# The third block's convolution filled and read three beats earlier in a hand-ordered Mamba and SwiGLU kernel

## The reference

```
x_in, res = split(x @ W_in)                    # 512 + 512 channels
u  = silu(causal_conv4(x_in))                  # 4 taps along the tokens, per channel
dt, B, C = split(u @ W_x)                      # 16, 16, 16
delta = softplus(dt @ W_dt + b_dt)
h[t] = exp(delta[t]*A) * h[t-1] + delta[t]*B[t]*u[t]      # 512 channels x 16 states
y[t] = sum over states of h[t]*C[t]  +  u*D
x1 = layernorm(x + (y * silu(res)) @ W_out)
out = layernorm(x1 + (silu(x1 @ Wg.T) * (x1 @ Wu.T)) @ Wd.T)      # hidden width 768
```

## Time and profile before

| what | us |
|---|---|
| median of 3 runs | 1822.53 |
| lowest and highest of them | 1819.36, 1822.55 |
| the profiled execution, its own time | 1828.11 |
| its span, first to last instruction | 1826.3 |
| mean granted TensorE clock | 0.990 |

### The profile page before, as it was taken

How to read it: one execution, slowest core, us unless ns; L and a number is a source line. 1 busy time by engine, 2 the same in 40 slices (tenths; PEclk the granted TensorE clock), 3 DMA queues, 4 the chain that set the end, 5 groups by cost and what they waited for, 6 DMA issues and landing times.

```text
span 1826.3 us, 32557 instructions
## 1 busy us (share of the span) xinstructions
PE 1692.8 (93%) x10128; PEld 1272.7 (70%) x10128; DVE 1683.3 (92%) x1958; ACT 1604.4 (88%) x2769; POOL 1606.6 (88%) x1629
## 2 busy tenths in 40 slices
PE   7979898999989899898999989899898999988788
PEld 3556676776767677676776767677676776767667
DVE  4989899999999999999999989999999999999994
ACT  4887989999898998989899898998989899898874
POOL 3989799998989899899998989999898998989870
PEclk9999999999999999999999999999999999999899
DMA  7312223222222223222232222313223232221110
GB/s 241 116 48 105 82 74 112 82 105 81 106 81 82 105 71 114 96 81 104 82 108 79 104 82 82 116 60 132 78 82 104 82 109 78 105 71 59 35 47 24
DMA packets 82108, 164.57 MB, mean 90 GB/s; under 512 B 10369, under 2 KB 28033, under 8 KB 81938
## 3 DMA queue, kind: packets, MB, share of 16 engines
q1 hardware_dynamic: 80498, 160.90, 25.5%
q10 hardware_dynamic: 1440, 1.58, 0.3%
HBM read 87.47 MB, written 8.91 MB: 53 GB/s over the span
## 4 chain that ended last, share of the span: by engine, by line
PE 74%; ACT 13%; POOL 4%; issue 4%; DVE 2%; DMA 1%; SPq 1%; DVEq 0%; ACTq 0%; POOLq 0%
PE ht_upper L737 11%; PE ht_lower L737 10%; PE y_upper L762 9%; PE fill L663 8%; PE fill L673 8%; PE fill L559 7%; PE fill L642 6%; POOL dbu L1237 3%; PE fill L612 3%; PE fill L595 3%; PE fill L574 3%; ACT gt L1103 2%; ACT da L1094 2%; DVE h L1432 2%; ACT z L988 2%
## 5 line engine op out<-in xcount | busy, mean ns | idle before, releaser
L1237 POOL TENSOR_TENSOR dbu<-du,brep 128x512 f32<-128x512 f32 x1024 | 1286.3, 1289 | 155.1 <-DVE h L1432 130.8
L1432 DVE TENSOR_TENSOR_SCAN h<-da,carry,dbu 128x512 f32<-128x512 f32 x960 | 1185.7, 1269 | 58.1 <-ACT da L1094 54.8
L1094 ACT ACTIVATE da<-delta,a_s 128x512 f32<-128x512 f32 x960 | 654.9, 692 | 78.2 <-DVE h L1432 71.2
L1103 ACT ACTIVATE gt<-ht_upper,ct 128x512 f32<-128x512 f32 x512 | 350.1, 684 | 69.7 <-PE ht_upper L737 66.5
L737 PE MATMUL ht_upper<-ident,h 128*128 128x128 f32 x2048 | 315.8, 277 | 70.4 <-ACT gt L1103 50.1
L737 PEld LDWEIGHTS ht_upper<-ident,h 128*128 128x128 f32 x2048 | 243.8, 142 | 196.0 <-issue 132.9
L1444 DVE SCALAR_TENSOR_TENSOR acc<-ht_lower,ct,acc 128x512 f32<-128x512 f32 x480 | 350.2, 730 | 14.9 <-PE ht_lower L737 13.4
L737 PE MATMUL ht_lower<-ident,h 128*128 128x128 f32 x2048 | 313.4, 276 | 26.1 <-DVE acc L1444 22.3
L762 PE MATMUL y_upper<-ident,gt 128*128 128x128 f32 x2048 | 309.7, 274 | 0.8 <-ACT kb L920 0.8
L737 PEld LDWEIGHTS ht_lower<-ident,h 128*128 128x128 f32 x2048 | 240.6, 142 | 79.2 <-DVE h L1432 37.7
L762 PEld LDWEIGHTS y_upper<-ident,gt 128*128 128x128 f32 x2048 | 246.4, 142 | 51.4 <-issue 38.2
(11 more groups left out here) (189 smaller groups left out, 1881.1 us busy)
## 6 DMA issues: line engine op xcount, KB each, us to landing
brep<-b_rows SPq DMA_DIRECT2D x127, 512.0 KB, 3.8
xs<-xin SPq DMA_DIRECT2D x242, 256.0 KB, 2.5
xr<-x SPq DMA_DIRECT2D x16, 512.0 KB, 5.4
xt_s<-x_t SPq DMA_DIRECT2D x15, 512.0 KB, 3.8
out<-xr SPq DMA_DIRECT2D x15, 512.0 KB, 2.9
win_s<-w_in SPq DMA_DIRECT2D x2, 512.0 KB, 5.2
h<-xin SPq DMA_DIRECT2D x4, 256.0 KB, 3.9
h<-xin ACTq DMA_DIRECT2D x4, 256.0 KB, 4.6
```

Source lines behind the costliest of these rows:

```text
L1094: nc.scalar.activation(dst[:, :], delta[:, par, m, :], ACT.Exp, scale=a_s[:, m, n:n + 1])\
L1103: nc.scalar.activation(gt[:, (n * UPPER + k) % GT, :], ht_upper[:, :], ACT.Copy, scale=ct[:, par, k, n:n + 1])\
L1237: nc.gpsimd.tensor_tensor(dbu[:, beat % DBU, :], du[:, par, m, :], brep[:, n // PIECE % 2, n % PIECE, :], ALU.mult).then_inc(dbu_ready, 1)
L1432: nc.vector.tensor_tensor_scan(h[:, n % 2, m, 0:T], da[beat % 2][:, :] if slot is None else da_ahead[:, slot, :], dbu[:, beat % DBU, :], c ...
```

## The change

The entry of conv2 in FILL_AT goes from beat 22 to 19 and in front of `res0`; its READ_AT goes from 25.5 to 22.5. All banks stay.

```diff
-           "o3": (18, 18, 18, 18), "res0": (20, 21), "conv2": (22,), "res1": (24, 25), "conv3": (26,), "x1t0": (26,),
+           "o3": (18, 18, 18, 18), "conv2": (19,), "res0": (20, 21), "res1": (24, 25), "conv3": (26,), "x1t0": (26,),
...
-READ_AT = {..., "xin2": 4.5, "conv2": 25.5,
+READ_AT = {..., "xin2": 4.5, "conv2": 22.5,
```

More of the change, by code:

```diff
@@ L57 @@
 GT = 4
-READ_AT = {"xin0": -2.5, "conv0": 11, "res0": 23.5, "xin1": 2.5, "conv1": 16, "res1": 27, "xin2": 4.5, "conv2": 25.5,
+READ_AT = {"xin0": -2.5, "conv0": 11, "res0": 23.5, "xin1": 2.5, "conv1": 16, "res1": 27, "xin2": 4.5, "conv2": 22.5,
            "res2": 31.5, "xin3": 9, "conv3": 28, "res3": 35, "dtb": 45, "ct": 47, "dt0": 48, "dt1": 50.5, "dt2": 53,
```

## The result

| | us |
|---|---|
| before, median of 10 | 1822.61 (1819.36 to 1825.63) |
| changed, median of 10 | 1828.13 (1826.16 to 1831.20) |
| ratio | 1.0025, 95% interval 1.0016 to 1.0033 |
| span in the profile, before and changed | 1826.3, 1825.5 |

The changed kernel is slower by 0.25%, some 4.6 us (2.9 to 6.0). The plain medians differ by 5.5 us, which is inside that interval; what follows uses the ratios unless it says otherwise. Two executions of the kernel before, timed beside e1 to e4, took 2758 and 6040 us and are left out of every ratio. The time is inside the predicted range, but on its slower side, and beyond the 0.2% within which I had put most of the chance. The two profiled executions, by themselves, say the opposite: 0.8 us less. That contradiction is the larger part of what follows.

What follows compares the result with a forecast made beforehand. No single bound: ACT and DVE hold each other, PE is packed at beat 19. Stall +4.9 and shift -5.7 gave -0.8, or +2.0 with half the waits; +0.7 over 1822.5 was taken: 1823.2 us, range 1818.0 to 1828.2.

Steps and rivals of the forecast that it cites:

- (a): PE, conv moved to beat 19: work up to 944.32 goes back 1.10 us; ht_upper of beat 22 makes gt 0.7 late.
- (b): ACT, conv2 read at beat 22.5: exp of beat 24 late, DVE waits about 0.4 us, bounds 0.22 to 0.55.
- (c): Beats 25.5 to 34: of the stall 0.35 us stays per turn, in 14 turns +4.9 us.
- the 0.57 us of relief: ACT at beat 25.5, where conv2's read is gone: 0.57 us gained, predicted to be spent in waiting.
- (d): Shift of block 3 released 3.5 us earlier: all four conv3 waits at beat 26 go, about -5.7 us.
- rival 1: Stall at exp of beat 24 alone, waits worth under 1.3 us: +4.9, to 1827.4 us; chance 0.23.
- (e): Turn 0, conv2 changes places with one in_proj matmul at beat 20: 0, bounds -0.5 and +0.5 us.

Runs made afterwards that it cites:

- e1: Changed kernel with conv2 still filled at beat 19 but read at 25.5 as before: 1827.58 us, ratio 1.0023 to before.
- e4: Kernel before without the shift of block 3 for chunks 1 to 15, output not the reference's: 1821.87 us, ratio 0.9997 to before.
- e3: Changed kernel with conv2's read back at 25.5 and the second half of res0 moved from beat 21 to 22: 1820.93 us, ratio 0.9982 to before.
- e6: Kernel before, unedited, profiled a second time: span 1819.2 us.
- e7: Kernel before, unedited, profiled a third time: span 1817.1 us.

## Why the prediction was right, and where its numbers were off

The time, 1828.13, is inside 1818.0 to 1828.2 by 0.07 us, which is luck. It is outside the forecast's own range, 1820.5 to 1825.5, and it came out as the slower kernel, to which I had given 0.23. The mechanism of every part on PE, ACT and DVE was found in the trace. The size of the stall came out too small, what stays of it too small by more, and the worth of the shift too large; all three errors hide a slower kernel.

- **(a) PE.** Right: the ht_upper of beat 22 is the one late. 1.15 us for 1.10: the four transposes that follow a conv take 0.50 (942.72 to 943.22) and not 0.43 or 0.44, and I had left that out. Shown by e1 to hold `gt` by itself.
- **(b) the stall at beat 24.** Mis-sized, 0.40 for 0.49. The prediction's own sum gives 947.78 - 947.41 = 0.37. 0.05 more is from (a). Another 0.04 is the step from `da` (done at 948.20) to its scan (948.24); I had counted such a step from ht_upper to `gt` and not here. That leaves 0.03 us, made up of still smaller things. My bounds, 0.22 to 0.55, held it.
- **(c) what stays of it.** This step failed. I subtracted 0.06 us of spare from 0.4 and took 0.35; it stays whole at 0.50. The 0.06 to 0.08 us between a scan's modelled end and `exp` is the step itself and no room: in the changed kernel, where `exp` is late and waits, the gaps are still 0.08 (952.49 to 952.57) and 0.06 (953.71 to 953.77). 14 x 0.50 = 7.0 us, not 4.9. That it goes through the SiLU stretch undiminished and that the 0.57 us of relief is spent in waiting was right: the bracket of 0.31 at 950.74 is that waiting.
- **(d) the shift.** Right on what happens (3.5 us earlier, no wait left), mis-sized on its worth. I took 5.7 us from one execution, with 2.9 as the lower end. By the ratio, 7.0 - 4.6 = 2.4 us was won (1.0 to 4.1); e3, the only kernel with this part alone, 3.3 (0.9 to 5.6); the three profiles of before had 5.8, 2.6 and about 1. Half of the profile's figure or a little less is what fits all but e4, whose 0.5 (a loss of 1.1 to a gain of 2.2) overlaps them at its edge.
- **The Trainium skill's rule** ("Runtime: NRT & Kernel Launch", "Instruction fetch mechanics": "mostly hidden"). I expected most of the waits in every execution because the instruction packet has its place in the program. This is the premise that failed. e6 and e7 have the same 85 packets in q8 and 2.6 and 0.9 us of the 5.8 us of waiting. The number of packets is the program's; where one falls beside the shift is not. The trace does not bear out that the fetch delays nobody either: all five landings at over 6 us have a packet in them. What moves the packet from one execution to the next stays open. In time the rule's side was nearer than mine: rival 1, where the waits are worth little, came closest, +4.9 against 4.6 (5.5 by the medians).
- **(e) turn 0.** I took 0 from the exchange of two matmuls. The profile shows -1.1 us, but this is the clock of the first trace, not the change: against e7 the changed kernel differs in turn 0 only at beat 8 (0.4 us), and not at beats 20 to 23, where the two matmuls are.
- **The sum of the profiled executions**, -0.8 predicted and -0.8 measured, agrees by accident. It is +7.0 for the stalls, -5.8 for the waits, -1.1 in turn 0, -1.4 from turn 15 on, and +0.5 of small things. Turn 0 is the clock of the first trace. So, it seems, is 0.6 us of turn 15: from 1717 to 1722 us the first trace has 0.66 and the changed kernel 1.00, and at 1719.36 DVE of the first trace waits 0.51 us for ht_lower, which it does not in the changed kernel. The other 0.8 us was not traced to a cause. Of the 9.2 us by which the first trace is longer than e7, 4.9 are waits of conv3 on `xs` and 2.6 are turn 0 and the start of turn 1, with the clock. So the profiled execution was above the others by its waits and by its clock; the prediction had weighed the waits alone.

So the forecast, +0.7 over the median, was off by its terms (c) and (d); with 7.0 and the half of 5.7 it would have been +4.2.

## What to carry to other kernels

In a list of work that is packed on one engine, what you move forward is paid by everything between its new and its old place; look at each item in there that another engine picks up, and price that item's delay on that engine, not the moved work. Here the first such items had room and a later one, the ht_upper of beat 22, had not; e3 took half of `res0` out of its way and won. A gap of 0.04 to 0.08 us between an end and the start that it releases was the hand-over in these traces, not spare. And a wait that is seen in one profiled execution is worth an average over several; profile the kernel before two or three times before you count on what its removal brings.

## What the runs showed of the hardware

Three traces of one and the same kernel differ by 9.2 us in span (1826.3, 1819.2, 1817.1), while each undisturbed turn agrees within 0.1 us. Two things differ. One is when four DMAs land: conv3 was short by nothing to 1.7 us in the same turn 1, and every landing over 6 us had a packet of the instruction queue in it, whose place moved by over 2 us between executions. The other is whether TensorE falls to 1.2 GHz in the sparsely filled turn 0 and at the start of turn 1. The first trace had three dips from 88 to 148 us, e6 two and e7 none, and the same 44 matmul records took 8.41 us for 6.81 where it did.
